# A fused attention and product-key expert layer: q and k's rests ahead of the gathers, similarities ahead of the weights, two gathers on VectorE

## What is computed

```python
q, k, v = split(x @ w_qkv.T)                      # 16 heads of 8
q, k = rope(rms_norm(q)), rope(rms_norm(k))
x = layernorm(x + softmax(causal(q @ k.T / sqrt(8))) @ v @ w_proj.T)

xn = rmsnorm(x, norm_w)
sim1, sim2 = xn @ w_q.T against the two halves of the keys     # 8 heads x 32 keys, twice
s1, i1 = top_k(sim1, 8);  s2, i2 = top_k(sim2, 8)
fs, pk = top_k(s1[:, None] + s2[None, :], 8)      # the best 8 of the 64 pairs
fi = (i1 * 32 + i2)[pk]                           # expert numbers, 0 to 1023
hidden = gelu(xn @ expert_down[fi]) * relu(fs)
x = layernorm(x + sum(hidden * expert_up[fi]))
```

## Time and profile before

| what | value |
|---|---|
| median of 3 runs | 1586.76 us (1584.29 to 1587.21) |
| the profiled execution | 1584.3 us, its span 1582.5 us |
| TensorE busy | 1347.7 us (85%) |
| VectorE busy | 1346.1 us (85%) |
| ScalarE busy | 906.5 us (57%) |
| GpSimd busy | 631.5 us (40%) |
| mean granted clock of TensorE | 0.916 of full speed |
| TensorE idle until GpSimd's third parts | 41.1 us in 15 waits |

### The profile page before, as it was taken

How to read it: one execution, slowest core, us unless ns; L and a number is a source line. 1 busy time by engine, 2 the same in 40 slices (tenths; PEclk the granted TensorE clock), 3 DMA queues, 4 the chain that set the end, 5 groups by cost and what they waited for, 6 DMA issues and landing times. The chain is left out here.

```text
span 1582.5 us, 55219 instructions
## 1 busy us (share of the span) xinstructions
PE 1347.7 (85%) x21008; PEld 984.0 (62%) x21008; DVE 1346.1 (85%) x6598; ACT 906.5 (57%) x1486; POOL 631.5 (40%) x1024
## 2 busy tenths in 40 slices
PE   5667888989898998989898998989899898878677
PEld 4333466666666766666676756666676666556567
DVE  5347699998889999988989998898989899698995
ACT  3656666666666666656666656666666666442110
POOL 4325163452717254461716255371815345050410
PEclk9887999999899999989999999999999999998667
DMA  3000000000000000000000000000000000000000
GB/s 87 8 7 8 8 10 8 16 2 9 16 9 16 9 16 9 16 2 9 16 9 16 9 15 3 9 16 9 16 9 16 2 16 2 2 16 1 9 2 17
DMA packets 30004, 18.80 MB, mean 12 GB/s; under 512 B 1840, under 2 KB 29232, under 8 KB 29744
## 3 DMA queue, kind: packets, MB, share of 16 engines
q1 hardware_dynamic: 29744, 15.23, 3.4%
HBM read 11.04 MB, written 4.19 MB: 10 GB/s over the span
## 5 line engine op out<-in xcount | busy, mean ns | idle before, releaser
L646 ACT ACTIVATE prob<-S 128x512 f32<-128x512 f32 x640 | 369.1, 596 | 139.8 <-PE S L813 130.2
L925 PE MATMUL G<-whot,onehot 128*128 128x16 bf16 x12288 | 381.9, 170 | 19.1 <-DVE whot L1305 15.9
L925 PEld LDWEIGHTS G<-whot,onehot 128*128 128x128 bf16 x12288 | 360.7, 97 | 50.9 <-DVE whot L1305 16.1
L1280 DVE TENSOR_TENSOR onehot<-lo_no,elo 128x1024 bf16<-128x1024 uint16 x512 | 347.8, 730 | 0.0
L455 POOL TENSOR_TENSOR gat<-qk_r,cosw 128x256 f32<-128x256 f32 x64 | 46.6, 729 | 558.9 <-DVE whot L1305 360.7
L508 POOL TENSOR_TENSOR gat<-gat,cande 128x1280 f16<-128x1280 f16 x64 | 171.8, 2684 | 99.1 <-DVE gat L1248 99.1
L813 PE MATMUL S<-causal,ident_b 128*128 128x128 bf16 x1024 | 194.2, 223 | 0.0
L811 PE MATMUL S<-qT,kT_even 128*128 128x512 bf16 (+3 forms) x512 | 142.3, 307 | 60.3 <-ACT prob L646 38.3
L825 PE MATMUL OV<-prob,vp 128*9 128x512 f32 (+3 forms) x2048 | 164.9, 466 | 29.7 <-ACT prob L646 24.2
L575 ACT ACTIVATE hid<-F 128x512 f32<-128x512 f32 x128 | 76.5, 598 | 180.5 <-PE F L881 180.5
L1226 DVE FIND_INDEX8 topi<-topv,sims 128x8 uint16<-128x32 f32 x1024 | 166.2, 185 | 0.1
(11 more groups left out here) (144 smaller groups left out, 2425.4 us busy)
## 6 DMA issues: line engine op xcount, KB each, us to landing
xa<-in_L_attn_x SPq DMA_DIRECT2D x16, 256.0 KB, 2.8
xr<-in_L_attn_x SPq DMA_DIRECT2D x16, 256.0 KB, 2.8
out<-r SPq DMA_DIRECT2D x15, 256.0 KB, 2.3
onehot<-in_L_ffn_expert_down SPq DMA_DIRECT2D x1, 512.0 KB, 5.7
up<-in_L_ffn_expert_up SPq DMA_DIRECT2D x1, 512.0 KB, 7.5
onehot<-in_L_ffn_keys SPq DMA_DIRECT2D x1, 256.0 KB, 4.7
out<-r SPq DMA_DIRECT2D x2, 128.0 KB, 1.8
onehot<-in_L_attn_w_qkv SPq DMA_DIRECT2D x1, 192.0 KB, 3.0
```

The source lines that it names most:

```text
L646: act.activation(dst, src, ACT.Exp, scale=SCALE).then_inc(exp_done.sem, 1)
L925: last = nc.tensor.matmul(bank[:, 16 * i:16 * i + 16], onehot[:, row, :], whot[:, t, w_part, :], start=(w_part == 0), stop=(w_part == 2))
L1280: return dve.tensor_tensor(onehot[:, row:row + 8, :].rearrange("p t (c i) -> p t c i", i=2), lo, e, ALU.is_equal)
```

## The change

Six edits:

- **GpSimd**: both `rests` stand ahead of gather 0, both `third_parts` ahead of candidates 2, and gathers 2 and 3 are gone.
- **VectorE** makes gathers 2 and 3 itself (`own_gather`), each right behind its `top_pairs`. They count on a semaphore of their own, on which `turn_numbers` of tiles 2 and 3 waits.
- **ScalarE**: `first_parts` after steps 12 and 14 (before 13 and 20), `second_parts` after steps 20 and 21 (before 23 and 24).
- **VectorE** normalises the second half of q and k between the top keys of tiles 0 and 1 (before: ahead of the pairs of tile 0).
- **TensorE**: `transpose_yi` and `project_similarities` stand ahead of the weights of their step.
- **VectorE**: one-hots 14 and 15 ahead of `squares_summed`, and one-hot 16 ahead of `norm2` instead of beside a root's step.

```diff
@@ GpSimd
-                    .then_inc(gat_done.sem, 1)
+                    .then_inc(gat_done.sem, 3 if t == 1 else 1)
@@
                 if late is not None:
                     candidates(late, 0)
                     candidates(late, 1)
-                    gather(late, 0)
                 if nxt is not None:
                     rests(nxt, 0)
                     rests(nxt, 1)
                 if late is not None:
-                    candidates(late, 2)
-                    gather(late, 1)
+                    gather(late, 0)
                 if nxt is not None:
                     third_parts(nxt, 0)
                     third_parts(nxt, 1)
                 if late is not None:
+                    candidates(late, 2)
+                    gather(late, 1)
                     candidates(late, 3)
-                    gather(late, 2)
-                    gather(late, 3)
@@ ScalarE
-                    if nxt is not None and n in (13, 20):
-                        first_parts(nxt, (n - 13) // 7)
+                    if nxt is not None and n in (12, 14):
+                        first_parts(nxt, (n - 12) // 2)
@@
-                    if nxt is not None and n in (23, 24):
-                        second_parts(nxt, n - 23)
+                    if nxt is not None and n in (20, 21):
+                        second_parts(nxt, n - 20)
@@ TensorE
-                pe.wait_ge(gat_done.sem, gat_done.value(b, t + 1))
+                done = gat_done if t < 2 else own_gat_done
+                pe.wait_ge(done.sem, done.value(b, t + 1))
@@
+                    if step == 7 and late is not None:
+                        transpose_yi(late)
+                    if late is not None and step in SIMS_STEPS:
+                        project_similarities(late, SIMS_STEPS.index(step))
                     if older is not None and step in WEIGHT_STEPS:
                         part = WEIGHT_STEPS.index(step)
                         weights(older, part)
@@ VectorE
+            def own_gather(b, t):
+
+                dve.wait_ge(hotc_done.sem, hotc_done.value(b, t + 1))
+                dve.tensor_tensor(gat[:, t % 2], gat[:, t % 2], cande[:, t % 2].rearrange("p h c -> p c h").unsqueeze(3)
+                                  .to_broadcast([P, NCAND, H, TOPK]), ALU.mult)\
+                    .then_inc(own_gat_done.sem, 3 if t == 2 else 1)
@@
-                one_hots(hot(10, 14))
+                one_hots(hot(10, 16))
                 if nxt is not None:
                     squares_summed(nxt)
-                one_hots(hot(14, 16))
@@
                     norm1_moments(late)
+                one_hots(hot(16, 17))
                 if oldest is not None:
                     norm2(oldest)
@@
-                    roots(turn, slice(first.start, last.stop), hot(16, 20))
+                    roots(turn, slice(first.start, last.stop), hot(17, 20))
@@
                 if late is not None:
                     top_keys(late, 0)
+                if nxt is not None:
+                    normalise(nxt, 1)
+                if late is not None:
                     top_keys(late, 1)
@@
-                if nxt is not None:
-                    normalise(nxt, 1)
@@
                     top_pairs(late, 2)
+                    own_gather(late, 2)
@@
                     top_pairs(late, 3)
+                    own_gather(late, 3)
```

More of the change, by code:

```diff
@@ L255, in attention_then_peer_layer @@
         gat_done = signal("gat_done", NT)
+        own_gat_done = signal("own_gat_done", NT)
         numbers_turned = signal("numbers_turned", NT)
@@ L981, in iteration @@
                             expert_outputs(older, range(2), OV, 4)
-                    if step == 7 and late is not None:
-                        transpose_yi(late)
                     if b is not None and u == 1 and g:
                         transpose_o(b, g - 1)
-                    if late is not None and step in SIMS_STEPS:
-                        project_similarities(late, SIMS_STEPS.index(step))
                     if b is not None and u == UNITS - 1 and g < NG - 1:
@@ L1348, in iteration @@
                 if nxt is not None or late is not None or oldest is not None:
-                    roots(turn, slice(first.start, last.stop), hot(16, 20))
+                    roots(turn, slice(first.start, last.stop), hot(17, 20))
                 else:
-                    one_hots(hot(16, 20))
+                    one_hots(hot(17, 20))
                 if late is not None:
```

## The result

| | before | changed |
|---|---|---|
| median | 1585.62 us (1584.29 to 1587.21) | 1561.14 us (1555.68 to 1563.22) |
| profiled execution | 1584.3 us | 1560.9 us, its span 1558.8 us |
| TensorE, VectorE busy | 85%, 85% | 85%, 88% |
| GpSimd busy | 631.5 us | 570.6 us |
| mean granted clock | 0.916 | 0.921 |

The ratio is 0.984, 95% interval 0.9812 to 0.9867: 1.6% faster. The forecast was 1553 with a range of 1534 to 1575, so the sign and the range held, and the gain was 24 us, not 34. In the changed kernel decode is L1270, the weights L926, the numbers L892, GpSimd's gather L510, VectorE's own L1256, its one-hots L1288 and L1313, the application of weights L1326.

A forecast was written before the change was run, and what follows sets the result against it. TensorE with its waits was taken to set the pace: 89.03 - 5.0 + 1.4 + 2.0 = 87.43 us an iteration, -29.3 over twelve, -33.8 with the edges; 1550.5 profiled, median 1553 us, range 1534 to 1575.

The forecast's parts named there:

- The stall, its wait and its slow clock: TensorE at L761 and step 27: 3.01 us stall, 0.39 wait and 1.6 slow clock go, -5.0 us an iteration.
- First parts, +1.4: ScalarE after steps 12 and 14: the second pair delays step 19's exponential and `attend` 1, +1.4 us an iteration.
- The clock over `attend`, +2.0: TensorE idling between steps 15 and 19 slows the clock over `attend` 1 in every iteration, +2.0 us.
- A second fall of the clock: Sign against the prediction: the clock falling at a second place in each iteration.
- The sum: 89.03 - 5.0 + 1.4 + 2.0 = 87.43 us an iteration, against a mean of 89.87.
- VectorE's own path, "at most 86.0": VectorE's path per iteration, at least 3.03 us shorter than the iteration because of its waits at decode, norm 2 and top keys.
- rival A: The clock holds: TensorE would need 85.4, VectorE's path of some 86.0 us is then longer; 1536 us, chance 0.17.
- Own gathers: Gathers 2 and 3 on VectorE: 1.5 us each, +3.0, against -3.46 from faster products and one-hots; VectorE gains 0.46 us.
- Similarities ahead, cost 0: Similarities ahead of TensorE's weights: L1318 will wait, but top keys wait anyway; nothing won or lost above 0.2 us.
- B: GpSimd becomes the thin spot: candidates 2 and gather 1 come late behind the third parts; 1571 us, chance 0.15.
- C: The clock, once down between steps 15 and 19, stays down until step 27; slower, 1603 us, chance 0.09.
- D: No change: the 3 us freed at L761 return as TensorE's waits for q and k copies; within 3 us of 1587, chance 0.07.

## Why the prediction was partly right

**The stall, its wait and its slow clock: right.** From the start of `attend` 1 to the transposes 14.52 us became 13.20: the 2.1 of the slow `attend` less the 3.4 of stall and wait. From there to `attend` 2, 6.76 became 5.32: 1.44 where 1.6 was forecast.

**First parts, +1.4: right in mechanism, somewhat low.** From the exponential of step 12 to `attend` 1, 10.12 us became 11.90, +1.78, and with the first parts back it was 10.1 again.

**The clock over `attend`, +2.0: right.** It fell there in every iteration and cost 2.1 us in nine of them, 1.4 to 2.0 in the other three.

**A second fall of the clock: not forecast**, named as what would prove the prediction wrong if it came in each iteration; it came in ten of the twelve. From `attend` 2 to the next iteration's first projection 22.10 us became 22.81, +0.71: 16 transposes take 1.93 us for 1.34, `attend` 3 takes 2.58 for 2.34. I don't know why it falls there now.

**The sum.** -1.32 - 1.44 + 1.78 + 0.71 and -0.1 elsewhere make -0.37 on 89.03, so 88.66; forecast was 87.43. Of the 1.23 missing 0.71 are the second fall, 0.38 the first parts, 0.16 and 0.08 the two terms above, less 0.1. Over the loop's mean the miss is (88.45 - 87.43) x 12 = 12.2 us; the edges gave 6.4, not 4.5. 12.2 - 1.9 = 10.3, and the profiled execution was 10.4 above its forecast.

**VectorE's own path, "at most 86.0": the step that failed.** I had added VectorE's three waits, 3.03 us, and taken them off the iteration. But these waits are for TensorE, which in turn waits for VectorE's `whot` in step 31, so they aren't spare: they are parts of a ring through both engines. The measure of a ring is the slack where it closes. In the kernel before, TensorE's row for step 31 was

```profile
881.11 0.75 PE L925 MATMUL G<-whot,onehot 128*128 128x16 bf16 x24
```

and `whot` was complete at 874.98 + 4.18 = 879.16: 1.95 us of slack, not 3.03. In the changed kernel it is 0.34. So even with the clock held over `attend` 1, as rival A had it, the time would not have come to 1536: the kernel with the output's rows moved shows it, where 3.45 us were lifted and nothing was won. The sum above therefore tells where the time of one iteration went, not what the time would be with one entry taken away. The forecast's own number did not hang on this step, since its 87.43 lay above the 86.0; rival A did, and so did every further repair.

**Own gathers: right in their own time, wrong in the saving set against it.** 1.49 us for 1.5, in 31 of 32. The one-hots came down from 3.67 to 2.49, as reckoned, and with the gathers back on GpSimd they take 4.0. But the 2.28 us at the three products had one iteration behind them: in the kernel before they took 4.18 in two iterations of three and 2.06 in the third, and with the gathers back on GpSimd they take 2.0 in nine of twelve, so most of this saving does not come from the move. What the first own gather did was to put 1.49 us ahead of `whot`: with it the slack at step 31 is 0.34, without it 2.01. The single-rate estimate of 1.49 us goes by a formula that the Trainium skill, page "VectorE: DVE Perf Modes", section "The TRN2 errata — SBUF-src ops pay a fixed extra latency per instruction", gives for fp32, and the trace now agrees with it.

**Similarities ahead, cost 0: right.** Apply 0 waits 1.09 where the top keys had waited 1.15, and undoing it changed nothing.

**Rivals.** B was close: its wait is what two of the experiments had, at 1.8 us an iteration, and the changed kernel misses it by 0.66 us. C did not come: the clock was up again by 854.2. D was partly true: the stall's 3 us were not all kept, though they went to ScalarE's stretch ahead of `attend` 1, not to the copies of q and k.

## What to carry to other kernels

Before pricing an edit on the engine that waits most, find every place where it takes something from another busy engine, and read the slack there (the producer's end against the consumer's start), even where no wait is listed: that slack caps the gain as long as the rest of the ring keeps its length. Waits of the second engine are no reserve when they are for the first one. When several different repairs all end at the same time, suspect two rings of equal length and lift both in one kernel, and look where the slow clock went: it can be part of what makes them equal.

## What I had not expected of the hardware

- Filling TensorE's waits with 48 useless small products (1.2 us) ahead of `attend` 1 kept the clock at 2.4 GHz over it in five of the twelve iterations. The time at 1.2 GHz fell by 44%, from about 109 to 61 us, and the kernel was no faster, since the products and the gaps that came with them cost as much.
- The clock's main fall went along with TensorE's idling: in the kernel before it stood at the wait of 3.01 us for the stack, in the changed kernel behind the waits of 1.07, 1.33 and 0.69 us, and in the kernel with the output's rows moved at the wait of 3.22 us for `whot`, 0.50 from 871.5 to 878.3, in each iteration. The second fall of the changed kernel, at step 39, has no such wait ahead of it. The one at `whot`:

```profile
871.50:878.30 6.80, 5.29 (x92) 4.70 (x94) 6.54 (x33) 2.12 (x4) 0.00 (x0) 0.50 0.01 4
```
